# Layer 3 of a decoder: the normalisation, transpose and gates of the cell moved into the attention's loop over the sequences

## What is computed

```python
# per sequence, B = 32, tokens 128, width 128
x = x + attention(layernorm(x))            # 16 heads of width 64, causal
xn = layernorm(x)                          # the cell's normalisation
# the cell takes queries from xn, keys and values from the context ctx
gates = concat([xn, ctx, ctx]) @ [Wi; Wf].T + [bi; bf]   # 8 + 8 gates per token
i, f = gates[..., :8], gates[..., 8:]
# log-sigmoid of f, running sums and running maxima over the tokens follow,
# then the weights exp(...), the products with the context, group norm, and x += ...
```

## Time and profile before

| | us |
|---|---|
| median of 3 runs | 3837.65 |
| lowest, highest | 3834.44, 3846.02 |
| the profiled execution, its time | 3835.66 |
| its span in the profile | 3833.8 |
| busy: TensorE, VectorE, ScalarE, GpSimd | 3465.1, 2688.0, 2437.2, 2075.0 |
| attention of layer 3, first gather to last addition | 2694.41 to 3154.08 |
| normalisation and gates, to the store of the gates | 3154.08 to 3191.78 |

### The profile page before, as it was taken

How to read it: one execution, slowest core, us unless ns; L and a number is a source line. 1 busy time by engine, 2 the same in 40 slices (tenths; PEclk the granted TensorE clock), 3 DMA queues, 4 the chain that set the end, 5 groups by cost and what they waited for, 6 DMA issues and landing times. The chain is left out here.

```text
span 3833.8 us, 90102 instructions
## 1 busy us (share of the span) xinstructions
PE 3465.1 (90%) x30069; PEld 2574.1 (67%) x30069; DVE 2688.0 (70%) x5870; ACT 2437.2 (64%) x9595; POOL 2075.0 (54%) x2606
## 2 busy tenths in 40 slices
PE   8989979988988999999889998899899998788897
PEld 5656645557776878888666665666688874456587
DVE  6857749977774767777688886644577754979822
ACT  6958944445452437777635991455688875688655
POOL 4534319977993433344366540275666635556744
PEclk9989999999999999999989998999999999999889
DMA  7013420010000000000000003135500003300078
GB/s 110 2 23 48 53 61 1 1 56 1 1 1 22 2 2 7 6 7 6 6 2 6 12 7 119 28 99 91 220 22 21 22 30 116 116 2 10 31 263 302
DMA packets 320103, 185.17 MB, mean 48 GB/s; under 512 B 214104, under 2 KB 289127, under 8 KB 318613
## 3 DMA queue, kind: packets, MB, share of 16 engines
q1 hardware_dynamic: 303716, 147.68, 14.2%
q0 software_dynamic: 13568, 27.36, 3.1%
q10 hardware_dynamic: 2370, 4.39, 0.3%
HBM read 131.43 MB, written 50.54 MB: 47 GB/s over the span
## 5 line engine op out<-in xcount | busy, mean ns | idle before, releaser
L3889 POOL DMA_INDIRECT l2f_b_xb<-l2f_tokens,l2f_inv x160 | 155.5, 972 | 174.8 <-issue 157.9
L2684 POOL TENSOR_TENSOR l1x_Sx<-l1x_Sx,l1x_sm 128x512 f32<-128x512 f32 x128 | 132.6, 1046 | 184.7 <-DVE l1x_sm L2890 184.7
L2684 POOL TENSOR_TENSOR l3a_Sx<-l3a_Sx,l3a_sm 128x512 f32<-128x512 f32 x128 | 133.4, 1043 | 129.8 <-DVE l3a_sm L2890 128.2
L3005 ACT ACTIVATE l1x_Sx<-l1x_Sx,l1x_nmx 128x128 f32<-128x128 f32 x512 | 199.0, 393 | 3.8 <-DVE l1x_nmx L2884 3.8
L1470 PEld LDWEIGHTS l0f_acc<-l0f_d_xk,l0f_d_Z 128*128 128x128 f32 x1024 | 124.7, 191 | 113.8 <-POOL l0f_d_Z L1438 112.8
L3005 ACT ACTIVATE l3a_Sx<-l3a_Sx,l3a_nmx 128x128 f32<-128x128 f32 x512 | 199.0, 392 | 0.1
L865 ACT ACTIVATE l3f_Pr<-l3f_S,l3f_nmx 128x128 f32<-128x128 f32 x512 | 182.5, 402 | 3.3 <-DVE l3f_nmx L795 3.3
L865 ACT ACTIVATE l2x_Pr<-l2x_S,l2x_nmx 128x128 f32<-128x128 f32 x512 | 183.9, 426 | 0.4 <-DVE l2x_nmx L795 0.4
L1350 ACT ACTIVATE l0x_Pr<-l0x_S,l0x_nmx 128x128 f32<-128x128 f32 x512 | 181.4, 403 | 3.1 <-DVE l0x_nmx L1267 2.6
L865 ACT ACTIVATE l0a_Pr<-l0a_S,l0a_nmx 128x128 f32<-128x128 f32 x512 | 182.6, 406 | 0.7 <-DVE l0a_nmx L795 0.7
L1470 PE MATMUL l0f_acc<-l0f_d_xk,l0f_d_Z 128*128 128x128 f32 x1024 | 144.5, 284 | 25.1 <-POOL l0f_d_Z L1438 24.9
(11 more groups left out here) (757 smaller groups left out, 11938.7 us busy)
## 6 DMA issues: line engine op xcount, KB each, us to landing
l3f_b_W<-in_l3f_we SPq DMA_DIRECT2D x72, 514.0 KB, 5.5
l3f_sorted<-l3a_blank SPq DMA_DIRECT2D x1, 17680.0 KB, 51.1
l3x_Mb<-l3x_dram_max SPq DMA_DIRECT2D x32, 512.0 KB, 4.3
l2f_results<-l2f_b_ys SPq DMA_DIRECT2D x40, 256.0 KB, 2.8
l2f_W<-in_l2f_w SPq DMA_DIRECT2D x1, 6144.0 KB, 25.9
l3f_b_xb<-l3f_sorted SPq DMA_DIRECT2D x72, 65.0 KB, 4.4
l0f_ew<-in_l0f_ew SPq DMA_DIRECT2D x1, 4096.0 KB, 13.2
l3f_XS<-l3f_results SPq DMA_DIRECT2D x8, 512.0 KB, 6.6
```

Of the source, the lines that this page charges most:

```text
L2684: pool.tensor_tensor(quad(Sx, s, q), quad(Sx, s, q), bcast_in(sm[:, s, 4 * q:4 * q + 4], P), ALU.mult).then_inc(w_done, 1)
L3005: ins = nc.scalar.activation(Sx[:, s, h, :], Sx[:, s, h, :], ACT.Exp, bias=nmx[:, s, h:h + 1], accum_out=sm[:, s, h:h + 1])
L3889: pool.indirect_dma_start(xb[:, j % 16, :], None, rows[:, :], bass.IndirectOffsetOnAxis(inv[:, j:j + 1], 0), bounds_check=None).then_inc(x ...
```

## The change

The block of `normalise_all` and the first part of the gates' block are gone. A new class `Gates` does the same work tile by tile in the attention's steps, and the attention is now called from inside `stage_l3_xattn`, so that `XT`, `CT`, `GT` are there. In step b: bn_stats and bn_aggr of tile b-1, right behind its last addition; the addition and the power on GpSimd, and the scale, of tile b-2; the transpose of tile b-3, and the gate products of tile b-4 on TensorE, in two unused quarters of the bank `TO`; the copy to `XT` of tile b-4 and the activation to `GT` of tile b-5 on ScalarE. Behind the last step up to four short ones drain this. The load of `wg`, `gb`, `CT` and `gn` is issued at the start of the attention instead of behind it, and ScalarE waits for all five before its first step. The square root on ScalarE becomes a power on GpSimd.

```diff
+class Gates:
...
+    def dve_step(self, dve, b):
+        m, r = b - 1, b - 2
+        if span(m):
+            wait(dve, self.x_done, m + 1)
+            wait(dve, self.rstd_done, m - 1)
+            self.nc.vector.bn_stats(self.stat[:, m % 2, :], tile_of(self.X, m)).then_inc(self.stats, 1)
+        if span(r):
+            wait(dve, self.rstd_done, r + 1)
+            wait(dve, self.turned, r - 1)
+            self.nc.vector.tensor_scalar(self.xn[:, r % 2, :], tile_of(self.X, r), self.mv[:, r % 2, 0:1], self.ve[:, r % 2, 1:2],
+                                         ALU.subtract, ALU.mult).then_inc(self.normed, 1)
+        if span(m):
+            wait(dve, self.stats, m + 1)
+            wait(dve, self.normed, m - 1)
+            self.nc.vector.bn_aggr(self.mv[:, m % 2, :], self.stat[:, m % 2, :]).then_inc(self.moments_done, 1)
+
+    def pool_step(self, pool, b):
+        r = b - 2
+        if span(r):
+            wait(pool, self.moments_done, r + 1)
+            wait(pool, self.normed, r - 1)
+            pool.tensor_tensor(self.ve[:, r % 2, 0:1], self.mv[:, r % 2, 1:2], self.C.eps, ALU.add).then_inc(self.var_eps, 1)
+            wait(pool, self.var_eps, r + 1)
+            pool.tensor_tensor(self.ve[:, r % 2, 1:2], self.ve[:, r % 2, 0:1], self.C.neghalf, ALU.pow).then_inc(self.rstd_done, 1)
+
+    def pe_step(self, pe, b):
+        g, r = b - 4, b - 3
+        if span(g) or span(r):
+            wait(pe, self.xnt_done, min(b + 2, NB))
+            wait(pe, self.x_done, min(b - 1, NB))
+            wait(pe, self.g_done, g)
+            wait(pe, self.copied, g + 1)
+        if span(g):
+            if g == 0:
+                pe.wait_ge(self.w_done, 1)
+            gates = self.TO[0:16, 3 * P:4 * P]
+            self.nc.tensor.matmul(gates, self.wg[:, 0, :], tile_of(self.XT, g), start=True, stop=False)
+            self.nc.tensor.matmul(gates, self.wg[:, 1, :], tile_of(self.CT, g), start=False, stop=True).then_inc(self.g_mm, 1)
+        if span(r):
+            wait(pe, self.normed, r + 1)
+            self.nc.tensor.transpose(self.TO[:, 2 * P:3 * P], self.xn[:, r % 2, :], self.C.ident).then_inc(self.turned, 1)
...
+    def act_step(self, act, b):
+        r, g = b - 4, b - 5
+        if span(r) or span(g):
+            wait(act, self.x_done, min(b - 1, NB))
+        if span(r):
+            wait(act, self.turned, r + 1)
+            self.nc.scalar.copy(tile_of(self.XT, r), self.TO[:, 2 * P:3 * P]).then_inc(self.copied, 1)
+        if span(g):
+            wait(act, self.turned, min(g + 2, NB))
+            wait(act, self.g_mm, g + 1)
+            self.nc.scalar.activation(tile_of(self.GT, g), self.TO[0:16, 3 * P:4 * P], ACT.Identity,
+                                      bias=self.gb[:, :]).then_inc(self.g_done, 1)
...
@@ -2726,6 +2806,8 @@
             if front and ahead(b):
                 ln.rstd(pool, b + 2, s, C)
+            if gates is not None:
+                gates.pool_step(pool, b)
             gather(b, 0)
@@ -2848,6 +2932,8 @@
                     project_v(nxt, 1 - s, n)
+            if gates is not None:
+                gates.pe_step(pe, b)
             if b + 2 < NB:
                 normed_T(b + 2, s)
@@ -2976,6 +3062,8 @@
                 quant.dve_step(dve, b)
+            if gates is not None:
+                gates.dve_step(dve, b)
         return step
@@ -3033,6 +3121,8 @@
                 copy_normed(nxt, 1 - s)
+            if gates is not None:
+                gates.act_step(act, b)
             if tail:
                 exps(prev, 1 - s, 3)
...
+                for b in range(NB + 1, NB + 4):
+                    hold_clock(nc, C, wide.S, 1)
+                    gates.pe_step(pe, b)
+                hold_clock(nc, C, wide.S, 2)
...
-            with nc.sbuf_tensor("l3x_XN", [P, NB * DM], F32) as XN:
-                normalise_all(nc, C, sems, "l3x_n", X, XN, turned=XT, beside=load)
             GT = sy("GT", [2 * HEADS, NB * P])
+            with ExitStack() as z:
+                stage_l3_attn(nc, C, sems, X, Gates(nc, C, z, X, XT, CT, GT, wg, gb), load)
```

More of the change, by code:

```diff
@@ L2664, in take @@
                     eng.wait_ge(sem, value)
+    if gates is not None:
+        gates.place(sems, TO, x_done, xnt_done)
     if quant is not None:
@@ L2811, in project_out @@
             wait(pe, num_done, 2 * b + 2)
+            if gates is not None:
+                gates.read(pe, b + 1)
             if quant is not None:
@@ L3064, in wide_head_attention @@
                  last={"tensor": (y_mm, NB), "vector": (x_done, NB), "scalar": (num_done, 2 * NB), "gpsimd": (w_done, 4 * NB)})
[L3067 to L3098, removed]
-            def _(act):
-                step = wide.scalar(act)
-                for b in range(-3, NB + 1):
-                    step(b)
-        sems.clear()
 def stage_l1_l2_attns(nc, C, sems, d, X):
@@ L4101, in stage_l2_ffn, with stage_l3_attn, _ @@
                             C.l2f_weight)
+def stage_l3_attn(nc, C, sems, X, gates, load):
+    with ExitStack() as x:
+        w, wf = C.big, C.big[:, 3, :].rearrange("p (c n) -> p c n", c=8)
+        wide = wide_head_attention(nc, C, sems, x, "l3a", X, w[:, 0, :], w[:, 1, :], w[:, 2, :], wf, 1.0 / 8,
+                                   back=(C.l2f_rows, C.l2f_idx, C.l2f_weight, C.l2f_back), gates=gates)
+        with nc.Block() as block:
+            @block.sync
+            def _(sp):
+                load(sp)
+                wide.sync(sp)
+            @block.gpsimd
+            def _(pool):
+                step = wide.gpsimd(pool)
+                for b in range(-3, NB + 1):
+                    step(b)
+                gates.pool_step(pool, NB + 1)
+            @block.tensor
+            def _(pe):
+                step = wide.tensor(pe)
+                hold_clock(nc, C, wide.S, 9)
+                for b in range(-3, NB + 1):
+                    step(b)
+                for b in range(NB + 1, NB + 4):
+                    hold_clock(nc, C, wide.S, 1)
+                    gates.pe_step(pe, b)
+                hold_clock(nc, C, wide.S, 2)
+            @block.vector
+            def _(dve):
+                step = wide.vector(dve)
+                for b in range(-3, NB + 1):
+                    step(b)
+                    if b == 1:
+                        gates.dve_start(dve)
+                gates.dve_step(dve, NB + 1)
+            @block.scalar
+            def _(act):
+                step = wide.scalar(act)
+                act.wait_ge(C.l3x_in, 80)
+                for b in range(-3, NB + 1):
+                    step(b)
+                for b in range(NB + 1, NB + 5):
+                    gates.act_step(act, b)
+        sems.clear()
 def stage_l3_tail(nc, C, sems, d, X):
@@ L4567 @@
 STAGES = [stage_l0_attn, stage_l0_xattn, stage_l0_ffn, stage_l1_l2_attns,
-          stage_l2_ffn, stage_l3_attn, stage_l3_tail]
+          stage_l2_ffn, stage_l3_tail]
 def build(nc, d, x_dram, out_dram, stages=None):
```

35 lines of the change are left out of this document (16 added, 19 removed).

## The result

| | before | after |
|---|---|---|
| median of 18 runs each, us | 3836.20 | 3848.66 |
| lowest, highest | 3831.24, 3846.74 | 3837.38, 3856.57 |
| the profiled execution, its time; its span | 3835.66; 3833.8 | 3839.61; 3837.8 |
| first gather to first addition | 46.79 | 48.49 |
| first to last addition | 412.59 | 451.22 |

The ratio of the times is 1.0024, interval 1.0016 to 1.0033: 9 us slower, under the 0.3% that tell a difference. It is not the ratio of the medians, which lie 12.5 us apart; the means lie 9.4 us apart. The stage itself is 9.6 us longer. The profiled execution shows only 4.0 us more because the code ahead of the stage, the same in both kernels, took 2688.67 us instead of 2694.41; in further executions of the changed kernel it took 2692.44 and 2691.43.

A forecast was written before the change was run, and what follows sets the result against it. TensorE was taken to be full at 13.35 us a step, with about no slack on VectorE and 0.91 on GpSimd. Steps 36.4 + start 1.5 - removed block 33.1 = +4.8 us on 3837.65: 3842 us, range 3822 to 3862.

The forecast's parts named there:

- The forecast case: Whole kernel: the time lands between 3833 and 3850 us, about 3842; chance 0.48.
- steps 4 to 27: Attention steps in which gathers are still issued: 0.6 + 0.6 + 0.15 = 1.35 us added to each, 32.4 us over 24.
- TensorE, 0.6 a step: Attention step, behind the V projection: two gate matmuls and one transpose, five records of 0.12, add 0.6 us, bounds 0.5 and 1.0.
- VectorE, 0.65 until the inversion: Between the addition to X and the old moments: bn_stats, scale and bn_aggr make the inversion 0.65 us later, bounds 0.5 and 0.9.
- GpSimd, 0.8: Ahead of the gather and quarter 3: an addition and a power on one column add 0.8 us, bounds 0.75 and 1.1.
- The old scale falls to 0.35: VectorE's scale of the next tile, 1.60 us beside gather and multiplication, takes 0.35 to 0.45 as the gather comes later.
- The stand before quarter 3, 0.6: TensorE waits 0.6 us before turning quarter 3, whose multiplication on GpSimd ends at t+6.59 where TensorE wants it at t+6.0.
- The collision, 0.15 on GpSimd: VectorE's joins start just ahead of the multiplication of quarter 3 and cost GpSimd 0.15 us a step.
- the joins go first: Slower rival: quarter 3 on GpSimd waits for all four joins, 1.4 us a step, 3872 us; chance 0.25 for 3850 to 3872.
- The start, 1.5: Attention start: the 2 MB context load beside the first gathers delays the first join 2.5 us; costs 1.5 us, bounds 0 and 5.
- The tail, 4.6: After the last addition: the remaining gate work of tile 31 and one block end take 4.6 us, bounds 3 and 8.
- TensorE alone sets the period: Faster rival: GpSimd's chain is not late, each step gets only 0.6 us, period 13.95, 3823 us; chance 0.24.

## Why the prediction was right, and where its steps were not

3842 was forecast, 3822 to 3862 the range, 3848.66 came; "within 0.3%" was the likeliest class and came. The forecast case is the one that happened. The change itself came out twice as large as forecast: +4.8 us for the stage, +9.6 measured. That the time still fell inside is owed to a range 40 us wide, and that the step sum came so near is partly luck, since errors cancelled: TensorE was 0.20 too low, the stand 0.03 too low, the collision 0.15 too high, which makes 1.43 of 1.35. The stage shows which terms were short.

| term | forecast | measured |
|---|---|---|
| steps 2 and 3 | 1.1 | 1.4 |
| steps 4 to 27 | 24 x 1.35 = 32.4 | 34.3 (1.43 each) |
| last five steps | 2.9 | 3.0 |
| start | 1.5 | 1.7 |
| block removed less new tail | -33.1 | -30.7 |

- **TensorE, 0.6 a step: low.** The records take 0.70 and the first starts 0.10 later behind the V projection than the transpose did before: 0.80. In the place where TensorE stood idle the period grew by 0.73, with nothing else late. I had priced five records at 0.12; a pair of gate products starts 0.23 after the one before, but the transpose stands 0.31 behind the second pair.
- **VectorE, 0.65 until the inversion: right.** t+1.37 against t+0.73, 0.64.
- **GpSimd, 0.8: right.** From the start of the old power to the gather it is 1.53 us (2945.40 to 2946.93) instead of 0.76: 0.77.
- **The old scale falls to 0.35: right**, 0.34. That it does so only because the gather comes later is shown by the kernel with GpSimd's part behind quarter 3 (2.00 us).
- **The stand before quarter 3, 0.6: right.** It is 0.63, by 0.66 at the turn (t+6.71 instead of t+6.05). Quarter 3 ended at t+6.56 where I said t+6.59; the turn started 0.15 after that, where I had allowed 0.05.
- **The collision, 0.15 on GpSimd: wrong, and harmless.** The multiplication kept its time, in all 81 instances between 2800 and 3100; VectorE was held instead, one join taking up to 1.69 us:
```profile
L2764 POOL TENSOR_TENSOR l3a_Sx<-l3a_Sx,l3a_sm x81: 1033/1047/1053, 2800.3 to 3096.2; 128x512 f32<-128x512 f32 x81
```
```profile
L2992 DVE SCALAR_TENSOR_TENSOR x_sbuf<-l3a_parts,l2f_weight,x_sbuf x84: 350/352/1691, 2800.1 to 3098.2; 128x128 f32<-128x128 f32 x84
```
  It is the first join of the four that is held, and it had started ahead of the multiplication, by 0.19 us in most steps and by 0.48 us in the longest case:
```profile
2947.86 1.40 DVE L2992 SCALAR_TENSOR_TENSOR x_sbuf<-l3a_parts,l2f_weight,x_sbuf 128x128 f32<-128x128 f32 x1
...
3051.38 1.69 DVE L2992 SCALAR_TENSOR_TENSOR x_sbuf<-l3a_parts,l2f_weight,x_sbuf 128x128 f32<-128x128 f32 x1
```
```profile
3051.86 1.05 POOL L2764 TENSOR_TENSOR l3a_Sx<-l3a_Sx,l3a_sm 128x512 f32<-128x512 f32 x1
```
  Both times it ended 0.16 behind the multiplication. This hold took back 1.05 of the 1.26 us that the short scale had won: the last key copy ends at t+10.26 (2952.12 + 0.68), not near t+9.5 as forecast. TensorE needs it only at t+11.02, the stand having moved that back too, so the hold reached nobody, which the kernel with the joins later confirms. It is why "the joins go first" did not happen.
- **The start, 1.5: right in size.** The first join came 9.77 us after the first gather instead of 6.58, 3.2 later where I had said 2.5, and 1.7 of these 3.2 us reached the first addition; other executions of the changed kernel gave 0.7 and 1.4, and kernels with the same start up to 2.5 (49.28). With the load moved away from the gathers the first join came at 6.57 us and the first addition at 46.79, as before. That edit moved ScalarE's wait for the loads too; in the changed kernel it can hardly have counted, since the last load had landed by 2698.6 (2689.51 + 9.1) and ScalarE's first copy began at 2702.46.
- **The tail, 4.6 with "4 to 6" as the sign of being right: wrong**, 7.0 from the end of the last addition. Two things were left out. The block ends with TensorE's two idle matmuls, 1.4 us (7.28 against 5.84 and 5.85 without them). And the last transpose does not follow its scale: TensorE first waits for ScalarE's copy of the tile before and its activation of the one before that (3190.58 to 3190.93), then issues the products, and turns at 3191.71, 1.1 us after the scale's end. (An idle matmul stands ahead of the products as well, with a modelled end of 3191.18 where they start. In the short step before it had ended at 3189.20, and they started at 3189.47, 0.26 us behind the activation.) I had added up the last tile's chain alone, not its place in the queue.
- **TensorE alone sets the period** (the faster rival, 13.95) needed less than 0.91 us added on the way to quarter 3; 1.42 were (quarter 3 ended at t+6.56 instead of t+5.14). Moving TensorE's part into the stand made it true, at 14.08.

The Trainium skill (SBUF — State Buffer, "Who interferes with whom") says that a VectorE instruction with two SBUF inputs contends with a GpSimd instruction that reads SBUF, and that issue order decides who blocks. By the profile's marks this trace does not agree on the order: the first join had started 0.19 us ahead of the multiplication, once 0.48 us, and it was the join that waited (1.40 and 1.69 instead of 0.35) while the multiplication took its 1.05. GpSimd's marks are rough, but 0.48 us is more than a whole join takes. In another stage of the kernel before it was the multiplication that grew, to 1.46. The join had started while GpSimd was issuing a gather (2946.93 to 2948.01), VectorE's instruction there beside a power of one column (1812.09 to 1812.63); whether that decides who waits is not shown.

## What to carry to other kernels

Work moved into a full pipeline costs its own time on the bound engine and, beyond that, whatever it pushes past another engine's slack; write down each loop's slack and spend the added time against it. If a stand remains, put the bound engine's part of the moved work into it: here that one move of three instructions took 16 us off the stage. Of a tail, add up the queue that the last item stands in and what the block does after it, and of a DMA that is moved, ask what its issuing engine waits for ahead of it.

## What the runs showed of the hardware

- A scale on VectorE from SBUF to SBUF that starts 0.26 to 0.65 us into GpSimd's issue of a gather does not run beside it: it ends when the gather and the multiplication behind it are through (1.60, 1.95, 2.00 us instead of 0.34). One that started 0.08 us into a gather (in the kernel with VectorE's part in mid-step) took 0.33. Started 0.21 us into GpSimd's power of one column, it took 0.34.
- A join (two SBUF inputs) runs at 0.35 us beside gathers. A join that had begun 0.19 us before a multiplication of 128 x 512 ended 0.16 us behind it (1.40), and the multiplication kept its 1.05: it never gave way in this stage.
- Two equal additions on one column of GpSimd, with no wait between, start 0.14 us apart; with a semaphore between an addition and a power the second starts 0.25 to 0.27 after the first.
- The time of code that is the same in all kernels varied by up to 11 us between profiled executions (2688.67 to 2699.69 ahead of the stage), while the stage's period was 14.77 in all three profiles of the changed kernel.
